# Own-attention scores in two row tiles, one step later, and one transpose for two batches' probabilities

## What is computed

```
x = x + xattn(layernorm(x), ctx)      # keys and values from ctx [8, 1601, 256]
x = x + attn(layernorm(x), causal)    # "own attention": 64 x 64 scores per head and batch
x = x + moe(layernorm(x))             # 8 experts of 256-1024-256, the best 2 weighted by softmax
```

```
qkv = y @ in_proj.T ;  q, k, v as [b, head, 64, 16] ;  q = q / 4
scores = where(causal, q @ k.T, -inf) ;  attn = softmax(scores) ;  out = (attn @ v) @ out_proj.T
```

## Time and profile before

| | |
|---|---|
| median of 3 runs | 660.2 us (658.1, 660.2, 660.26) |
| profiled execution, device time | 658.37 us |
| its span in the profile | 656.6 us |
| TensorE busy | 628.2 us, 96% |
| VectorE busy | 472.9 us, 72% |
| ScalarE busy | 329.8 us, 50% |
| GpSimd busy | 305.1 us, 46% |
| granted TensorE clock, mean | 0.995 |

### The profile page before, as it was taken

One profiled execution on the slowest core, in us unless ns is written; L12 is line 12 of the kernel. 1 busy time (PEld: TensorE's weight loads), 2 busy tenths in 40 slices (PEclk: granted clock), 3 DMA queues, 4 the chain that ended last, 5 costly groups with the idle time before them and its releaser, 6 DMA issues.

```text
span 656.6 us, 15592 instructions
## 1 busy us (share of the span) xinstructions
PE 628.2 (96%) x6312; PEld 530.1 (81%) x6312; DVE 472.9 (72%) x878; ACT 329.8 (50%) x541; POOL 305.1 (46%) x386
## 2 busy tenths in 40 slices
PE   6989999999989999998999999988989999999997
PEld 4778878868877877887887887767889999999997
DVE  4887767757697687587876867587777667756653
ACT  4355655555555564546465546474554444444421
POOL 2138788898696798687779868200000000000000
PEclk9999999999999999999999999999979999999999
DMA  6312011010010010011100000333003311330000
GB/s 183 137 46 57 27 51 27 27 51 27 27 38 15 27 52 26 26 27 51 27 27 26 2 1 2 128 132 129 1 4 125 129 50 80 128 128 0 0 0 33
DMA packets 13285, 34.11 MB, mean 52 GB/s; under 512 B 1563, under 2 KB 10532, under 8 KB 11044
## 3 DMA queue, kind: packets, MB, share of 16 engines
q1 hardware_dynamic: 13188, 33.19, 15.2%
q0 software_dynamic: 32, 0.01, 0.0%
HBM read 32.67 MB, written 0.52 MB: 51 GB/s over the span
## 4 chain that ended last, share of the span: by engine, by line
PE 69%; DVE 14%; POOL 8%; issue 5%; ACT 2%; DMA 1%; SPq 0%; POOLq 0%; DVEq 0%; ACTq 0%
PE bank L1211 44%; POOL prob_sum L494 8%; PE bank L1400 7%; PE bank L1220 6%; PE bank L1386 3%; PE bank L1281 3%; DVE maxes L927 2%; DVE prob_sum L494 2%; DVE ctx_lo L478 1%; DVE k_lo L908 1%; PE bank L1336 1%; DVE shift L869 1%; ACT k_hi L630 1%; PE bank L1308 1%; DVE qbd L873 1%
## 5 line engine op out<-in xcount | busy, mean ns | idle before, releaser
L494 POOL TENSOR_TENSOR prob_sum<-probs,prob_sum 128x256 f32<-128x256 f32 x336 | 273.9, 846 | 61.6 <-ACT probs L743 56.1
L743 ACT ACTIVATE probs<-bank 128x1024 f32<-128x1024 f32 (+1 forms) x104 | 106.7, 1026 | 110.1 <-PE bank L1400 80.9
L927 DVE TENSOR_REDUCE maxes<-bank 128x1 f32<-128x400 f32 (+1 forms) x256 | 129.4, 564 | 16.5 <-PE bank L1281 16.0
L725 ACT ACTIVATE h_raw<-bank,b_sb 128x512 f32<-128x512 f32 (+2 forms) x72 | 46.2, 642 | 104.9 <-PE bank L1211 101.0
L908 DVE SCALAR_TENSOR_TENSOR k_lo<-bank,bias_sb,k_hi 128x400 fp32r<-128x400 f32 (+2 forms) x64 | 40.4, 631 | 47.6 <-ACT k_hi L630 47.5
L1211 PE MATMUL bank<-w_hi,h_hi 128*128 128x256 f32 x256 | 73.7, 288 | 0.5 <-DVE h_lo L1146 0.5
L1211 PE MATMUL bank<-w_lo,h_hi 128*128 128x256 f32 x256 | 73.1, 286 | 0.0
L1211 PE MATMUL bank<-w_hi,h_lo 128*128 128x256 f32 x256 | 73.1, 285 | 0.0
L1220 PE MATMUL bank<-probs,v_sb 128*32 128x128 f32 (+1 forms) x1664 | 67.0, 279 | 2.0 <-ACT probs L743 1.9
L1145 DVE CAST h_hi<-h_raw 128x512 fp32r<-128x512 f32 (+2 forms) x72 | 28.5, 396 | 55.9 <-ACT h_raw L725 54.5
L1211 PE MATMUL bank<-wv_hi,ctx_hi 128*128 128x256 f32 (+1 forms) x208 | 65.1, 313 | 2.8 <-DVE maxes L927 2.6
(11 more groups left out here) (155 smaller groups left out, 1386.7 us busy)
## 6 DMA issues: line engine op xcount, KB each, us to landing
raw<-in_w SPq DMA_DIRECT2D x16, 1024.0 KB, 6.8
ctx_raw<-in_ctx_t SPq DMA_DIRECT2D x16, 400.0 KB, 3.6
ctx_raw<-in_ctx_t SPq DMA_DIRECT2D x8, 402.0 KB, 3.7
ctx_raw<-in_ctx_t SPq DMA_DIRECT2D x8, 399.0 KB, 3.6
w_sb<-in_w_t SPq DMA_DIRECT2D x1, 1280.0 KB
w_raw<-in_w_t SPq DMA_DIRECT2D x2, 256.0 KB, 4.7
result<-x_all SPq DMA_DIRECT2D x4, 128.0 KB, 1.9
x_all<-in_x SPq DMA_DIRECT2D x1, 384.0 KB, 4.1
```

The lines of the kernel that those rows point to most:

```text
L494: ins = engine.tensor_tensor(prob_sum[0:ROWS[k], cols], probs[0:ROWS[k], s % 2, cols], acc[0:ROWS[k]], ALU.add)
L725: nc.scalar.activation(h_raw[:, c % 2, 0:width], bank[:, at, 0:width], ACT.Gelu, bias=b1_sb[:, bass.ds(e, 1), c:c + 1].rearrange("p a b -> ...
L743: nc.scalar.activation(probs[0:ROWS[k], s % 2, :].rearrange("p (g n) -> p g n", g=G), bank[0:ROWS[k], score_bank(b, k):score_bank(b, k) + ...
L927: nc.vector.tensor_reduce(maxes[:, g * PAIRS + j, c:c + 1], src[:, 0:width], AX.X, ALU.max).then_inc(read_dve, 1)
```

## The change

The own scores s0 and s1 become two units each, u = 0 and 1. The first waits for its bank and returns; the second issues all matmuls: for each group of heads and i = 0, 1, one matmul on partitions 0 to 63 into the bank of the first unit and one on partitions 64 to 127 into the bank of the second. Each has 64 rows where it had 128; their number stays 8 a batch. `step_units` puts them ahead of the K and chain units, behind the M units, which from the third on stand behind the key tile's scores. They come a step later: s0 in step 9 (was 8) and s1 in 11 (was 10), in the last tile 8 and 10 (were 7 and 9). DVE reads each with one instruction of 256 elements a partition.

`soft` is laid out as [128, 8 pairs, 2 batches, 64] so that both batches of a pair of heads are 128 neighbouring columns. One transpose turns both: t0 and t1 (one for each group of heads) with 4 transposes of 128 x 128 each take the place of the four units, in step 14 (were 12 and 13), in the last tile 13 (were 11 and 12). They wait for the division of both batches. ACT copies each with one instruction of 128 partitions. o0 moves from step 14 to 15, beside o1. `GATE_BANKS` gives the tail's gt and b2 the banks that they had.

```diff
-CHAIN_AT = {3: ["y1"], 5: ["xt1"], 6: ["qk", "v"], 8: ["s0"], 10: ["s1"], 12: ["t00", "t01"], 13: ["t10", "t11"],
-            14: ["o0"], 15: ["o1"], 17: ["y2"], 19: ["xt2"], 20: ["router"], 24: ["gt"], 25: ["b2"]}
+CHAIN_AT = {3: ["y1"], 5: ["xt1"], 6: ["qk", "v"], 9: ["s0"], 11: ["s1"], 14: ["t0", "t1"],
+            15: ["o0", "o1"], 17: ["y2"], 19: ["xt2"], 20: ["router"], 24: ["gt"], 25: ["b2"]}
...
+CHAIN_AT_LAST = {2: ["y1"], 4: ["xt1"], 5: ["qk", "v"], 8: ["s0"], 10: ["s1"], 13: ["t0", "t1"], 14: ["o0", "o1"],
+                 16: ["y2"], 18: ["xt2"], 19: ["router"], 23: ["gt"], 24: ["b2"]}
+CHAIN_ALONE = {1: ["y1"], 2: ["xt1"], 3: ["qk"], 5: ["s0", "s1", "v"], 7: ["t0", "t1"],
...
-    others += [(c, 0) for c in chain]
-    row = m + others
+    others += [(c, 0) for c in chain if c not in ("s0", "s1")]
+    row = m + [(c, r) for c in chain if c in ("s0", "s1") for r in range(ROW_TILES)] + others
...
-        soft = sb("soft", [P, 2, G * PAIRS, Q])
+        soft = sb("soft", [P, G * PAIRS, 2, Q])
...
-                    bi, g = int(kind[1]), int(kind[2])
-                    rows = slice(bi * Q, bi * Q + Q)
-                    nc.scalar.activation(probs2[rows, g * 512:g * 512 + 512], src[rows, :], ACT.Copy)\
-                        .then_inc(read_act, 1)
+                    g = int(kind[1])
+                    nc.scalar.activation(probs2[:, g * 512:g * 512 + 512], src, ACT.Copy).then_inc(read_act, 1)
...
-                    nc.vector.tensor_tensor(soft[:, int(kind[1])], src.rearrange("p (n k) -> p n k", k=Q),
-                                            causal_sb[:, :].unsqueeze(1).broadcast_to([P, G * PAIRS, Q]),
+                    each = PAIRS // ROW_TILES
+                    nc.vector.tensor_tensor(soft[:, :, int(kind[1]), :].rearrange("p (g r i) q -> p r g i q", g=G, r=ROW_TILES)[:, u],
+                                            src[:, 0:G * each * Q].rearrange("p (g i q) -> p g i q", g=G, i=each),
+                                            causal_sb[:, :].unsqueeze(1).unsqueeze(1).broadcast_to([P, G, each, Q]),
...
                     for g in range(G):
-                        for j in range(PAIRS):
-                            m = g * PAIRS + j
-                            ins = nc.tensor.matmul(dst[:, m * Q:m * Q + Q],
-                                                   own_queries[:, g, 2 * j:2 * j + 2, :].rearrange("p s q -> p (s q)"),
-                                                   k2_t[:, g, bi * Q:bi * Q + Q], start=True, stop=True)
+                        for i in range(each):
+                            for r in range(ROW_TILES):
+                                rows, j = slice(RT * r, RT * r + RT), each * r + i
+                                at = (g * each + i) * Q
+                                ins = nc.tensor.matmul(bank[:, units.bank_of(n - ROW_TILES + 1 + r), at:at + Q],
+                                                       own_queries[rows, g, 2 * j:2 * j + 2, :].rearrange("p s q -> p (s q)"),
+                                                       k2_t[rows, g, bi * Q:bi * Q + Q], start=True, stop=True)
+                                if g == G - 1 and i == each - 1 and r < ROW_TILES - 1:
+                                    ins.then_inc(filled, 1)
...
-                    pe.wait_ge(rows2_ready, 2 * t + bi + 1)
+                    pe.wait_ge(rows2_ready, 2 * t + 2)
                     for j in range(PAIRS):
-                        turned, own_rows = dst[bi * Q:bi * Q + Q, j * P:j * P + P], soft[:, bi, g * PAIRS + j, :]
-                        if bi == 0:
-                            ins = nc.tensor.transpose(turned, own_rows, ident[:, :])
-                        else:
-                            ins = nc.tensor.matmul(turned, own_rows, ident[:, :], start=True, stop=True)
+                        ins = nc.tensor.transpose(dst[:, j * P:j * P + P],
+                                                  soft[:, g * PAIRS + j].rearrange("p b q -> p (b q)"), ident[:, :])
```

More of the change, by code:

```diff
@@ L155, in __init__ @@
                      for n in range(len(order))]
+        if banks is ALONE_BANKS:
+            for n, kind in enumerate(order):
+                self.bank[n] = GATE_BANKS.get(kind, self.bank[n])
     def counts(self, n):
@@ L673, in own_exponentials @@
                         act.wait_ge(soft_ready, 2 * t + bi + 1)
-                        nc.scalar.activation(soft[:, bi], soft[:, bi], ACT.Exp).then_inc(soft_exp_done, 1)
+                        nc.scalar.activation(soft[:, :, bi, :], soft[:, :, bi, :], ACT.Exp).then_inc(soft_exp_done, 1)
             def step(units, s, t, b, parity):
@@ L956, in after_units @@
             def after_units(units, s, *kinds):
-                for n, kind, _ in units.at[s]:
-                    if kinds and kind not in kinds:
+                for n, kind, u in units.at[s]:
+                    if kinds and kind not in kinds or kind in ("s0", "s1") and u < ROW_TILES - 1:
                         continue
@@ L1151, in alone @@
                     unit(TAIL, m, kind, u, TT - 1, B, 0)
-                    if kind == "s0":
+                    if kind == "s0" and u == ROW_TILES - 1:
                         after_units(TAIL, s, "s0")
@@ L1320, in unit @@
                     units.wait_read_act(pe, read_act, "qk")
+                    if u < ROW_TILES - 1:
+                        return
+                    each = PAIRS // ROW_TILES
                     for g in range(G):
-                        for j in range(PAIRS):
-                            m = g * PAIRS + j
-                            ins = nc.tensor.matmul(dst[:, m * Q:m * Q + Q],
-                                                   own_queries[:, g, 2 * j:2 * j + 2, :].rearrange("p s q -> p (s q)"),
-                                                   k2_t[:, g, bi * Q:bi * Q + Q], start=True, stop=True)
+                        for i in range(each):
[7 more added lines that the diff above has]
+                                    ins.then_inc(filled, 1)
                 elif kind[0] == "t":
-                    bi, g = int(kind[1]), int(kind[2])
-                    pe.wait_ge(rows2_ready, 2 * t + bi + 1)
+                    g = int(kind[1])
+                    pe.wait_ge(rows2_ready, 2 * t + 2)
                     for j in range(PAIRS):
-                        turned, own_rows = dst[bi * Q:bi * Q + Q, j * P:j * P + P], soft[:, bi, g * PAIRS + j, :]
-                        if bi == 0:
-                            ins = nc.tensor.transpose(turned, own_rows, ident[:, :])
-                        else:
-                            ins = nc.tensor.matmul(turned, own_rows, ident[:, :], start=True, stop=True)
+                        ins = nc.tensor.transpose(dst[:, j * P:j * P + P],
+                                                  soft[:, g * PAIRS + j].rearrange("p b q -> p (b q)"), ident[:, :])
                 elif kind in ("o0", "o1"):
@@ L1340, in unit @@
                     rows = slice(bi * Q, bi * Q + Q)
-                    units.wait_read_act(pe, read_act, f"t{bi}1")
+                    units.wait_read_act(pe, read_act, "t1")
                     nc.tensor.matmul(dst[:, 0:E], ones_bf[:, :], ident_bf[:, 0:E], start=True, stop=True)
```

15 lines of the change are left out of this document (6 added, 9 removed).

## The result

The changed kernel takes 651.5 us (median of 4 runs, 648.75 to 652.71) against 660.2: a ratio of 0.988, 95% interval 0.985 to 0.990. The profiled execution took 651.14 us with a span of 649.2. The forecast was 649.2, range 645 to 655.

What follows compares the result with a forecast made beforehand. TensorE, busy 96% of the span, was taken as the bound, with DVE and POOL equally full in the middle tiles' first half. Gains 5.0 + 4.4 + 0.7 = 10.1 us off 658.37 gave 648.3; 0.9 added made 649.2, range 645 to 655.

Steps and rivals of the forecast that it cites:

- Scores in row tiles: Own scores: two overlapping row tiles take 0.95 us a batch instead of 1.81, 0.86 less for each of 8 units.
- Rival A: Own scores in two row tiles do not overlap; gain 7.8 us, so 651.5 us; chance 0.13.
- Mode switches: TensorE changing row tiling around the own scores: 0 in the tiles, no more than 0.2 us in the tail.
- Transposes: Turning the probabilities: 24 instructions (2.68 us) become 8 taking 0.9 us, saving 1.8 for each of 4 tiles.
- DVE's reads: DVE reading the own scores in two instructions: 0.13 us more a batch, 0.26 a tile.
- Order: Scores, exponentials and divisions at later steps: TensorE waits 0 to 0.3 us for the exponential ahead of step 12.
- Middle tiles: Tiles 1 and 2: POOL's and DVE's queues limit the gain to 2.5 us each, 5.0 together.
- Last tile: Last tile: DVE and POOL have gaps, so TensorE's time counts; gain 4.4 us, bounds 2.7 and 4.5.
- Tail: Tail: transposes wait for DVE's last division; gain 0.7 us, with about 2.9 us of waiting before them.
- rival B: Tail: TensorE's clock falls after its 2.9 us pause, costing 2.7 us, so 652 us; chance 0.15.
- Sum: Whole kernel: middle tiles, last tile and tail together gain 10.1 us, giving 648.3 us for the profiled execution.

Runs made afterwards that it cites:

- e1: Changed kernel with the own scores' matmuls of rows 0 to 63 issued before those of rows 64 to 127, instead of alternating; 650.5 us (0.986).
- e5: Changed kernel with the unit v moved from step 6 to step 13 in the middle tiles; 649.9 us (0.989).
- e6: Changed kernel with half of POOL's sums left out behind each batch's first key tile; step 8 to 16 of tile 1 went from 32.96 to 30.45 us.
- e7: Kernel before with half of POOL's sums left out behind each batch's first key tile; step 8 to 16 of tile 1 went from 35.36 to 33.64 us.
- e12: Changed kernel run once more without any edit; 650.0 us (0.987).
- e4: Changed kernel with the first expert's hidden chunk 6 issued ahead of the tail's transposes; 649.2 us profiled, timed runs 656.4 to 660.2 us (0.989).
- e10: Changed kernel with TensorE products that nobody reads put into the tail's waits; 645.9 us (0.983).
- e2: Kernel before with only the transposes changed, full-row scores staying in their old steps; 651.7 us (0.988).
- e3: Kernel before with only the scores changed to two row tiles in the new steps, four turning units kept; 652.8 us (0.989).
- e11: Changed kernel with unread products in the tail's waits and v moved to step 13 in the middle tiles; 646.8 us (0.982).

## Why the prediction was right, point by point

**Scores in row tiles**: forecast 0.95 a pair, measured 0.93 to 1.04. Right; they overlap. Rival A did not come true. e1 took half of the overlap away (1.51 a pair), and at that its price was 0 in the middle tiles, where A had 0.3 for all of it. "Row tiles of fp32 are not in the trace" passed over a nearer row than the column tiles: the key tile's scores also alternate two row tiles of 64 rows, and their pairs start 0.12 apart, 0.06 an instruction, by which 16 come to 0.94. From the kernel before:

```profile
173.90 0.28 PE L1400 MATMUL bank<-qbd_hi,k_hi 64*128 64x256 f32 x2
174.02 0.28 PE L1400 MATMUL bank<-qbd_lo,k_hi 64*128 64x256 f32 x2
```

**Mode switches**: the 0.22 us that the forecast took for a switch (176.69 to 176.91) is none: scores and V both have 128 rows there, and in the changed kernel, where the scores have 64, the same two instructions are again 0.22 apart. The term was put at 0, so nothing hung on it. **Transposes**: forecast 0.9, measured 0.96. **DVE's reads**: 0.13 more, measured 0.08 (0.76 against 0.68). **Order**: ACT's exponential of s0 cost TensorE 0.16 ahead of step 12 (at 188.17, behind ACT's copy of V), inside the 0 to 0.3, and `qbd2` for s1 nothing. The forecast lacked the 0.35 of waiting for the pair's second bank.

**Middle tiles**: forecast 2.5 each. The two bounds taken from POOL's and DVE's rows were the right ones: denominators 3.4 us earlier was forecast, and it is 3.3 (2.68 from 200.48 to 197.80, plus the 0.67 by which this execution was later at step 8). `own_heads` 3.3 earlier, forecast 3.2 to 3.6. Tile 1 gained 2.4. e5, e6 and e7 show the bound at work. Tile 2 gained 1.3, and that is the one step of the forecast that failed: I had it as a copy of tile 1, and had looked for falls of the clock only in the tail. What the runs show in its place is 2.4 less 1.05 for a fall behind the new waits of step 14, present in two of four profiles with the same work up to there (changed and e12, not e4 and e10).

**Last tile**: forecast 4.4, measured 4.0. e2 loses there 1.32 of the 1.42 us that its two score units take longer on TensorE, e3 2.19 of 2.19 (the transposes' work and a stop of 0.36), e1 only 0.56 of 0.85: of the three tiles it is the one where TensorE's time counts. The missing 0.4 is mostly the scores': they took 1.70 and 1.81 here before (389.82 to 391.52, 397.40 to 399.21) and 1.04 after, a saving of 1.4 where I had 1.7.

**Tail**: forecast 0.7, measured 0.3. DVE's chain is as I had it (a wait of 2.73 us, forecast 2.9), but the fall of rival B came (chance 0.15) and cost 1.4, where B had 2.7. B had also read its price off too short a fall: 5.4 us stood for what lasted 6.8. That some of the gain is left is luck, since the second fall was half as long as in the kernel before and gave 0.8 back; 0.3 + 1.4 - 0.8 = 0.9 is an estimate of what the tail would have gained with that one fall as before. e10 bears the prices out: 3.2 us for both falls of the changed tail.

**Sum**: forecast 10.1; the stretches give 8.0; with the clock held the kernels are 10 us apart. Of the 2.1 us missing, 1.2 are tile 2's (1.05 of them its fall of the clock), 0.1 tile 1's, 0.4 the last tile's size and 0.4 the tail's. The sum's 648.3 for the profiled execution plus these 2.1 and the 0.7 of the later start are the 651.1 measured. The mechanism was right, and most of what is missing is the clock's. I had put 0.9 us on top of the sum for the median, which came out only 0.4 above the profiled execution; by luck this hid half a microsecond of the miss.

The Trainium skill (TensorE: Matmul & The Clock Gate, the HAM clock gate) says that pauses in matmul work let the clock fall to half. The trace agrees in its direction, twice over: the falls at 304 and at 461 stand behind waits that the change made (0.33 and 0.82 us in tile 2's step 14) or lengthened (2.73 us). The one at 475 stands behind waits that the kernel before has too. By the same page (LDWEIGHTS) a weight load takes its time by columns and not by rows. The trace agrees: in e1, where one row tile is alone, instructions of 64 rows start 0.11 us apart, as those of 128 rows do (1.81 / 16 = 0.113), and the pair's 1.51 us come from the part in which the two row tiles overlap.

## What to carry to other kernels

Where three engines are all full in a stretch, an operation removed from one is worth the distance to the next one's row, and that distance can be read off beforehand: the last busy end of each engine ahead of the point where they meet. The cheapest gain may then be where the second engine's unbroken row begins: moving the v product out of the step in which POOL waited gave 0.8 to 0.9 us a tile, more than the row tiles add there to the transposes alone (43.82 less 43.34, 0.48 us). And time saved on TensorE that turns into waiting can cost part of what it saves, or all of it, by the clock (1.05 us of 2.4 in tile 2, 1.4 in the tail); twenty unread products in the tail's four waits gave 3.2 us in the stretch that they fill. The fastest here is e10, with e11 equal within the scatter.

## What the runs showed of the hardware

- A stretch of 45 us repeats to 0.1 us between kernels and executions, and most of the scatter of a few us goes with falls of TensorE's clock: the kernel before took 655.9 to 657.0 us at a mean of 0.999 and 659.7 to 661.6 at 0.992.
- The same wait of 1.9 us in the last batch was followed by a fall in some kernels and by none in others; so was the same pause in tile 2's step 14 in executions with the same work up to there.
- A fall of 3.4 us cost 1.05 us in tile 2 and 1.4 to 1.7 in the tail.
- Matmuls of 64 rows start 0.11 us apart in one row tile, as with 128 rows, and 0.06 apart when two row tiles take turns; in e1 the second row tile's began while the first's were still starting (10 under way in 0.35 us, against 6).
- DVE's lateness of 1.72 us at the transposes of tile 1 went to 0.22 when POOL's additions were halved, with the same DVE instructions: its operations of two tensors took up to a quarter less time.
